# A depthwise convolution stage: Silu in one activation, taps over padded rows, another split between two engines

## The reference

```
xz = x @ in_proj_w.T
xh, z = jnp.split(xz, 2, axis=-1)
xc = jax.lax.conv_general_dilated(transpose(xh), conv_w, (1, 1), 'SAME', feature_group_count=DI)   # 3 x 3, depthwise
xc = jax.nn.silu(xc + conv_b[None, :, None, None])
x_flat = xc.reshape(B, DI, L)                              # rows after rows: U in the kernel
x_t = jnp.transpose(xc, (0, 1, 3, 2)).reshape(B, DI, L)    # columns after columns: UT
...                                                        # projections, a scan in four directions, a layer norm
y = y * jax.nn.silu(z)
return y @ out_proj_w.T
```

## Time and profile before

| | us |
|---|---|
| median of 3 runs | 4313.52 |
| lowest and highest run | 4308.7, 4328.05 |
| span of the profiled execution | 4322.2 |

### The profile page before, as it was taken

The page is one execution under the profiler, slowest core; times in us unless marked ns, Lnnn a source line. Parts: engine busy times, 40 slices in busy tenths (PEclk is TensorE's granted clock), DMA queues, the critical chain, the costliest instruction groups (busy, mean ns, idle before and its releaser), DMA issues. The chain is left out here.

```text
span 4322.2 us, 110119 instructions
## 1 busy us (share of the span) xinstructions
PE 3375.4 (78%) x46784; PEld 1688.2 (39%) x46784; DVE 3524.7 (82%) x3560; ACT 2718.5 (63%) x4416; POOL 1598.8 (37%) x1151
## 2 busy tenths in 40 slices
PE   6788873157777776317777778868999999999998
PEld 4476631012222223101222222553566566666553
DVE  5555476989999967789999996759988888888882
ACT  2365628845555544865555543534899999999995
POOL 0122220079999961009999995000000000000000
PEclk9799986568888887657888877977999999999999
DMA  5334203433232210353223321451221212222211
GB/s 130 83 67 75 54 18 91 145 79 79 71 76 71 66 49 10 112 146 74 72 65 77 76 61 39 126 153 41 56 56 56 64 56 56 64 56 56 56 41 49
DMA packets 160560, 309.95 MB, mean 72 GB/s; under 512 B 69592, under 2 KB 105752, under 8 KB 156101
## 3 DMA queue, kind: packets, MB, share of 16 engines
q1 hardware_dynamic: 159124, 301.24, 27.0%
q10 hardware_dynamic: 944, 1.67, 0.2%
HBM read 194.44 MB, written 107.83 MB: 70 GB/s over the span
## 5 line engine op out<-in xcount | busy, mean ns | idle before, releaser
L2323 DVE TENSOR_REDUCE l3a_mx<-l3a_mx 128x2 f32<-128x768 f32 x1296 | 1165.1, 952 | 160.2 <-PE l3a_mx L2222 156.1
L2289 ACT ACTIVATE l3a_p<-l3a_s 128x384 f32<-128x384 f32 x2592 | 1181.5, 492 | 113.2 <-PE l3a_s L2236 105.7
L1545 POOL TENSOR_TENSOR l_scan_sc<-l_scan_s,l_scan_repc 128x768 f32<-128x768 f32 x576 | 1032.3, 1837 | 5.9 <-DVE l_scan_s L1523 5.7
L1487 ACT ACTIVATE l_scan_da<-l_scan_da,l_k_a 128x768 f32<-128x768 f32 x576 | 503.9, 875 | 627.7 <-PE l_scan_da L1407 627.6
L2236 PE MATMUL l3a_s<-l3a_q,l3a_k 125*32 125x384 f16 x10368 | 802.1, 327 | 5.8 <-DMA l3a_q<-l3a_m 3.9
L2222 PE MATMUL l3a_mx<-l3a_k,l3a_q 124*32 124x384 f16 x10368 | 672.0, 334 | 57.4 <-DMA l3a_q<-l_qx 30.4
L1407 PE MATMUL l_scan_dup<-l_scan_du,l_k_pick 96*128 96x512 bf16 (+1 forms) x1152 | 347.2, 390 | 317.6 <-DMA l_scan_dt<-l_dtp 159.1
L2248 PE MATMUL l3a_o<-l3a_p,l3a_vh 128*32 128x288 f32 x6912 | 568.7, 405 | 0.8 <-issue 0.5
L1536 POOL TENSOR_TENSOR l_scan_bup<-l_scan_dus,l_scan_repb 128x768 f32<-128x768 f32 x192 | 352.6, 1837 | 484.6 <-DMA l_scan_repc<-l_bcp 484.6
L2190 POOL TENSOR_TENSOR l3a_norm<-l3a_out,l3a_spread 128x576 f32<-128x576 f32 x24 | 34.5, 1437 | 1342.1 <-DMA l3a_spread<-l_inverses 1342.1
L1407 PE MATMUL l_scan_da<-l_scan_dt,l_k_pick 96*128 96x512 bf16 (+1 forms) x1152 | 340.6, 384 | 156.1 <-DVE l_scan_s L1523 152.6
(11 more groups left out here) (215 smaller groups left out, 4295.3 us busy)
## 6 DMA issues: line engine op xcount, KB each, us to landing
l3a_q<-l_qx SPq DMA_DIRECT2D x96, 486.0 KB
l_scan_du<-l_dup SPq DMA_DIRECT2D x144, 144.0 KB
l_scan_dt<-l_dtp SPq DMA_DIRECT2D x138, 144.0 KB
l_scan_repb<-l_bcp SPq DMA_DIRECT2D x48, 384.0 KB
l_scan_repc<-l_bcp SPq DMA_DIRECT2D x46, 384.0 KB
l_dtp<-l_prep_high_t SPq DMA_DIRECT2D x16, 432.0 KB, 3.1
l_dup<-l_prep_high_u SPq DMA_DIRECT2D x16, 432.0 KB, 3.1
l_dtp<-l_prep_middle_t SPq DMA_DIRECT2D x16, 432.0 KB, 3.1
```

What stands on the lines that cost most here:

```text
L1487: act.activation(da_ps[st % 2][:, 0:TC], da_ps[st % 2][:, 0:TC], ACT.Exp, scale=A[:, column:column + 1]).then_inc(exped, 1)
L1545: pool.tensor_tensor(SC[:, st % NSC, :], S[:, n, :], REPC[k % 2][:], ALU.mult).then_inc(weighted, 1)
L2289: act.activation(P[:, k % NP, third * SW:(third + 1) * SW], s_ps[u % NS_PS][:, 0:SW], ACT.Exp)\
L2323: dve.tensor_reduce(MX[:, qt % (NB * KT), 2 * pair:2 * pair + 2], mx_ps[n % NR][:, :, 0:RG], AX_X, ALU.max)\
```

## The change

The stage is rewritten in four respects.

1. **Silu.** ACT's own Silu function replaces the chain of Exp, Ln and Exp. For z it reads the projected strip in PSUM and writes the gated strip. For u it reads the taps' sums and writes U, and a second Silu reads the same sums in exchanged order and writes UT, so the final copy is gone. The work is done by strip (PE's) and by unit (DVE's), not by image.
2. **Taps.** `conv` now has rows of 50 positions like `pad`, so that a DVE tap is one contiguous run of 16 x 50 - 2 = 798 positions in place of 16 rows of 48. The two positions at each row's end are computed and not used.
3. **Split.** DVE has five units (ten strips), PE two strips. POOL makes the nine diagonal matrices, and clears only the border of `pad` by four small memsets; ACT doesn't wait for them any more, DVE and PE do.
4. **Weights and stores.** The three loads move into `LateConstants.load`, ahead of its seven others, in the stage before. The stage no longer waits for the stores of U (`ssm_prepare` does, at its end), and U of the first image is stored earlier.

The core of the diff:

```diff
-            e = s.sb("e", [DI, B, L])
+        flat = s.sb("pad", [DI, B * (H + 2) * PADW])
+        pad = flat[:, :].rearrange("p (b h w) -> p b h w", b=B, w=PADW)
-        PE_STRIPS = [(1, r) for r in range(2 * PH, H, PH)]
-        DVE_UNITS = [(0, 0), (0, 2 * PH), (0, 4 * PH), (1, 0)]
+        DVE_UNITS = [(0, 0), (0, UNIT), (0, 2 * UNIT), (1, 0), (1, UNIT)]
+        PE_STRIPS = [(1, 2 * UNIT), (1, 2 * UNIT + PH)]
...
             @block.gpsimd
             def _(pool):
-                pool.memset(pad[:], 0.0).then_inc(padded, 1)
+                pool.memset(pad[:, :, 0, :], 0.0).then_inc(padded, 1)
+                pool.memset(pad[:, :, H + 1, :], 0.0).then_inc(padded, 1)
+                pool.memset(pad[:, :, 1:H + 1, 0:1], 0.0).then_inc(padded, 1)
+                pool.memset(pad[:, :, 1:H + 1, PADW - 1:PADW], 0.0).then_inc(padded, 1)
+                pool.wait_ge(loaded, 48)
+                for k in range(9):
+                    pool.tensor_scalar(diag[:, k, :], eye[0:DI, 0:DI], cw[:, k:k + 1], None, ALU.mult)\
+                        .then_inc(diag_made, 1)
...
+                def gate_z(n):
+                    b, r = strips[n]
                     act.wait_ge(z_ready, n + 1)
+                    act.activation(z[:, b, r * W:r * W + STRIP], z_ps[n % 3][:, 0:STRIP], ACT.Silu).then_inc(z_gated, 1)
+                def gate_unit(j):
+                    b, r = DVE_UNITS[j]
+                    act.wait_ge(tapped, j + 1)
+                    c = tapped_rows(b, r)
+                    act.activation(image_of(U[:, b, :])[:, r:r + UNIT, :], c, ACT.Silu).then_inc(gated, 1)
+                    act.activation(turned_home(b, r, UNIT), c.rearrange("p h w -> p w h"), ACT.Silu).then_inc(turned, 1)
+                def gate_strip(j):
+                    b, r = PE_STRIPS[j]
+                    act.wait_ge(taps_summed, j + 1)
+                    c = c_ps[j % 2][:, 0:STRIP]
+                    act.activation(U[:, b, r * W:(r + PH) * W], c, ACT.Silu, bias=cb[:, 0:1]).then_inc(strip_gated, 1)
+                    act.activation(turned_home(b, r, PH), c.rearrange("p (h w) -> p w h", w=W), ACT.Silu,
+                                   bias=cb[:, 0:1]).then_inc(strip_turned, 1)
+                unit_after = {10: 0}
+                unit_after_z = {4: 1, 10: 2}
...
                 for b, r in DVE_UNITS:
                     dve.wait_ge(placed, placed_for(b, r + UNIT))
-                    c = image_of(conv[:, b, :])[:, r:r + UNIT, :]
+                    c = conv[:, b, r * PADW:(r + UNIT) * PADW - 2]
                     for k in range(9):
-                        src = pad[:, b, r + k // 3:r + k // 3 + UNIT, k % 3:k % 3 + W]
+                        at = (b * (H + 2) + r + k // 3) * PADW + k % 3
+                        src = flat[:, at:at + UNIT * PADW - 2]
...
     def load(self, sp):
         t, pre = self.t, self.pre
+        sp.dma_start(self.cw_in[:], t[pre + "in_wT"].rearrange("(k p) n -> p k n", p=CP)).then_inc(self.conv_loaded, 16)
+        sp.dma_start(self.cw[:], t[pre + "conv_w"]).then_inc(self.conv_loaded, 16)
+        sp.dma_start(self.cb[:], t[pre + "conv_b"]).then_inc(self.conv_loaded, 16)
```

More of the change, by code:

```diff
@@ L912, in _, with place @@
             def _(pool):
-                pool.memset(pad[:], 0.0).then_inc(padded, 1)
-                for b in range(B):
-                    pool.wait_ge(z_exped, b + 1)
-                    pool.tensor_scalar(ez[:, b, :], ez[:, b, :], 1.0, E_MOST, ALU.add, ALU.min).then_inc(z_raised, 1)
+                pool.memset(pad[:, :, 0, :], 0.0).then_inc(padded, 1)
[6 more added lines that the diff above has]
+                        .then_inc(diag_made, 1)
             @block.scalar
             def _(act):
[L920 to L928, removed]
+                def place(n):
+                    b, r = strips[n]
                     act.wait_ge(x_ready, n + 1)
@@ L932, in _ @@
                        .then_inc(placed, 1)
-                act.wait_ge(loaded, 48)
-                for n, (b, r) in enumerate(strips):
+                def gate_z(n):
+                    b, r = strips[n]
                     act.wait_ge(z_ready, n + 1)
[L936 to L950, removed]
@@ L961, in _ @@
-                for b in range(B):
-                    act.wait_ge(gated, b + 1)
-                    act.activation(image_of(UT[:, b, :]), U[:, b, :].rearrange("p (h w) -> p w h", w=W), ACT.Copy)\
-                       .then_inc(turned, 1)
-                act.wait_ge(turned, B)
+                    act.activation(z[:, b, r * W:r * W + STRIP], z_ps[n % 3][:, 0:STRIP], ACT.Silu).then_inc(z_gated, 1)
[5 more added lines that the diff above has]
+                    act.activation(turned_home(b, r, UNIT), c.rearrange("p h w -> p w h"), ACT.Silu).then_inc(turned, 1)
@@ new lines, in _ @@
+                unit_after_z = {4: 1, 10: 2}
+                for n in range(n_s):
+                    if n in unit_after:
+                        gate_unit(unit_after[n])
+                    place(n)
+                for n in range(n_s):
+                    if n in unit_after_z:
+                        gate_unit(unit_after_z[n])
+                    gate_z(n)
+                gate_strip(0)
+                gate_unit(3)
+                gate_strip(1)
+                gate_unit(4)
+                act.wait_ge(turned, len(DVE_UNITS))
@@ L1074, in _ @@
                 sp.wait_ge(low_stored, 32 * UNITS)
+                sp.wait_ge(late.u_stored, 16 * B)
             @block.tensor
@@ L2429, in build @@
                         group_norm(nc, f"gn{layer}", X, XN, group_mean, preload=late.load, stats=stats)
[L2430 removed]
+                        ssm_conv(nc, pre + "conv", XN, late, U, UT, z_dram, u_dram, eye)
                     ssm_prepare(nc, pre + "prep", t, pre, U, UT, dt_dram, du_dram, bc_dram, late)
```

79 lines of the change are left out of this document (28 added, 51 removed).

## The result

| | before | after |
|---|---|---|
| median, us | 4317.34 (4 runs) | 4253.7 (4 runs) |
| lowest and highest run | 4308.7, 4328.05 | 4251.46, 4258.35 |
| span of the profiled execution | 4322.2 | 4249.7 |

The changed kernel is faster, by about 1.5 per cent: the ratio of its runs to those of before is 0.9854, with a 95% interval from 0.9833 to 0.9876. That is 63.6 us by the medians and, by the interval, between 54 and 72 us.

The account below looks back on a forecast made before the run. It took each convolution stage as a chain ending at a barrier, filled by no engine. Savings of 37.3 and 35.9 us, less 1 given back, made 72 us off 4313.5: 4241.5 us, range 4230 to 4260.

Parts of the forecast that it names:

- the forecast's own spread: Whole kernel: 4230 to 4252 us, from the units' bounds and the 10 us between timed runs of before.
- POOL in DVE's way: Rival, chance 0.14: POOL's diagonals at 1.2 us each, four falling into DVE's first unit, some 6 us a layer; 4254 us.
- no better taps: Rival, chance 0.10: tap 1.055 us, exchanged Silu 2.8 ns an element, weights 3 us late; about 7.5 us a layer, 4257.
- What bounds the stage: Convolution stage: a chain ending at a barrier, no engine filling it; 54.9 us in place of 92.26 and 90.79.
- DVE's five units set the end: End of the taps: DVE's last sums at 640.5, PE's strips at about 629.5 and 635.5, 5 us to spare.
- PE's own sum: PE in layer 1: projections through at about 623.5, under 2 us lost waiting for ACT, strips 5.85 us each.
- The size of a unit: DVE's unit of contiguous taps: 0.97 us a tap, 8.85 us a unit, 44.3 us for five.
- The upper bound: DVE's unit at most 9.5 us, from the old tap scaled by its elements, 1.055 us.
- The first tap: DVE's first tap: 7.29 us after the stage's start, at 596.24 in place of 600.62 in layer 1.
- Silu: ACT's gating: 0.82 ns an element and 0.17 us fixed; a unit's U 0.80 us, UT 1.48, together 2.3.
- Given back in the next stage: ssm_prepare: weights queue behind U's last store, 0.5 us a layer (0 to 3); Exp's table load covered by waiting.
- The total: Whole kernel: 72 us less than the 4313.5 us median, giving 4241.5 us.

Follow-up runs that it names:

- e_split: The changed kernel with the old split, four units on DVE and four strips on PE; stages 64.3 and 63.2 us against 58.56 and 57.60.
- e_imm: The changed kernel with the taps' weights and bias as numbers in the instruction, not SBUF columns (sums wrong); stages 55.26 and 55.52 us against 58.56 and 57.60.
- e_rows: The changed kernel with DVE's taps again over 16 rows of 48 in the padded layout; stages 57.22 and 56.46 us against 58.56 and 57.60.
- e_loads: The changed kernel with the three loads issued again at the convolution stage's start; stages 61.9 and 60.8 us against 58.56 and 57.60.
- e_zsilu: The kernel before with only z gated by one Silu out of PSUM; stages 87.9 and 87.4 us against 92.26 and 90.79.
- e_usilu: The kernel before with only u gated by one Silu per whole image, exchanged copy kept; stages 83.4 and 81.6 us against 92.26 and 90.79.
- e_warm: The changed kernel with unread PE products ending group_norm (four) and starting ssm_prepare (two); stages 55.6 and 57.3 us against 58.56 and 57.60.
- e_best: The changed kernel with row taps, three 24-row DVE units, three PE strips and unread PE products; stages 54.4 and 53.0 us, median 4243.9 us.

## Why the prediction was right, and where it was off

The direction and the mechanism were right, and the gain was 63.6 us in place of 72. The 4253.7 us lie above the forecast's own spread (4230 to 4252) and inside the range because this had been widened for two rivals. One of them, POOL in DVE's way, named 4254 and didn't happen; that the numbers meet is chance. The other, no better taps, had 1.055 us for a tap, and 1.046 was measured where the forecast had 0.97.

- **What bounds the stage**: right. The stage is a chain behind a barrier, and what came off it came off the whole: the stages lost 66.9 us and the rest of the program kept its length within the spread.
- **DVE's five units set the end, PE is ahead**: right, by 5.6 us (638.4 against 644.0). e_split shows the other side. PE's own sum was too short: its projections were through at 626.65 and not at 623.5, since it waited 1.78 us for ACT and the 20 products behind the wait took 8.38 us, part of them at the clock's lower level. DVE hid that.
- **The size of a unit**: the term that was off. The sum took 0.97 us for a tap, from the idea that the 75 ns between the old tap and a plain operation were its 16 rows. The trace had them in the column of weights (e_imm) and no cost of rows (e_rows). A unit takes 9.50 us in place of 8.85, five of them 3.25 us more, which is nearly all of the 3.7 us by which layer 1's stage is longer than forecast (58.6 against 54.9). The upper bound, 9.5, was just reached. In layer 2 the stage was 2.7 us longer, since the clock rose earlier there (0.77 already in the window from 2.7 to 5.7 us after the start) and the first tap with it.
- **The first tap**: 7.76 us into the stage in layer 1 and 6.80 in layer 2, against 7.29. The preload is worth 3.2 us a layer (e_loads), less than the 4.4 and 2.9 taken together.
- **Silu**: right in ACT's cost an element. The exchanged one took 1.63 in place of 1.48 us, the pair 2.38 in place of 2.3. PSUM's exchanged reads were cheaper than taken.
- **POOL in DVE's way**: didn't happen. A diagonal took 0.52 us against the 0.5 taken; the last ended at 594.1, before the first tap at 596.68. So what a diagonal costs beside the taps was not measured. The rival's own sum is not borne out by its terms either: four diagonals of 1.2 us are 4.8 us and not 6. That POOL's additions held DVE up is shown by e_zsilu, where the fourth unit is free.
- **Given back in the next stage**: PE's restart came 3.14 us after the stage's start in place of 2.93. Over all traces whose next stage has no work added it came after 3.1 to 4.3 us with the new stage and after 2.8 to 3.0 with the old, so 0.1 to 1.5 us are given back there; that it is the store ahead of the weights is likely, but not shown. DVE's first addition there came 1.5 and 0.9 us later after the start (18.4 and 17.9 against 16.9 and 17.0), but the other traces spread from 17.0 to 18.8 with the new stage and from 17.3 to 17.8 with the old, so most of that is spread. It didn't reach the next marks, where the difference is 0.1 us.
- **The total**: 4241.5 against 4253.7. Of the 12 us, 6 are the stages (73 forecast, 67 measured), 4 are the median of before, which was 4313.5 with three runs and 4317.3 with four, and the last 2 are within the runs' spread: the timed runs of before differ by 19 us, not by the 10 that the prediction says.

What each part brought, in one layer: z's Silu 4, u's 9, the split 5.7, the preload 3.3, contiguous taps -1.2, diagonals 0. That is 21 of 33.5 us, but the parts depend on each other and don't simply add up. With both Silus, u's would start behind PE's fourth strip, which ACT had copied 61.8 us after the start in e_zsilu; the two Silus and the exchanged copies took 12.1 us in e_usilu, and 1.05 to 2.4 us follow. That makes 74.9 to 76.2 us, so the two Silus together should be worth some 16 to 17 us and not 13 (an estimate; not run). The rest should be the work by strips and units in place of whole images, above all that the exchanged copy of 8.1 us no longer stands behind everything, and that the stage doesn't wait for U's last store, which SP issued only at 645.05. Neither was tried alone: both are argued, not shown. The split could bring its 5.7 only with z's chain gone, since in the kernel before ACT's queue was later than PE.

## What to carry to other kernels

Before you credit a saving to the shape of an operand, compare rows that differ in nothing else; a column of weights in SBUF cost DVE here what looked like the price of broken rows. Where a stage ends at a barrier, write down for each engine when it would be through, and price a removed wait by the second latest of them, an engine's own queue included: the largest stall in the old trace, 13.9 us, was worth 4 at most. When a program's runs differ by 10 us from layers that a change doesn't touch, measure the stage by its own marks.

## What the runs showed of the hardware

- DVE reads no faster from one run of elements than from 16 rows of 48: 1046 ns for 798 and 1015 for 768, one slope of 1.04 ns an element, up to 1415 ns for 1152.
- In the two DVE operations of a tap, each per-partition column in place of a number costs 60 ns (1046 to 986 with one, 692 to 573 with two).
- ACT pays for a wide step in SBUF on either side, 1630 ns reading and 1531 writing against 844 for 768 elements, and nothing for one in PSUM, 566 against 577 for 384 read exchanged.
- The Trainium skill, "SBUF — State Buffer" (Who interferes with whom), says that a DVE instruction with two SBUF inputs waits for the whole of a POOL instruction that reads SBUF. The two traces agree: 8002 ns for a tap beside POOL's addition, 8.37 us for all eight taps without it.
- Products that nobody needs, some 5 us of them ahead of a stage, brought PE's granted clock to 1.00 for the projections in one stage (e_warm, layer 1); in two, layer 2 of e_warm and of e_best, it was at 1.00 when the stage started, fell to 0.50 some 1 us later and was up again 3 us after that; in one it stayed at 0.50 (e_best, layer 1).
- The clock can fall behind a short wait: after 1.6 to 1.8 us in which PE waited for ACT amid z's projections, the next 20 products of 384 columns took 6.69 us in six stages, 8.38 in three and about 10 in three. After waits of 0.6 to 1.2 us (e_rows, e_imm) they took 6.69 in all four. In the changed kernel's layer 1 the granted clock was 1.00 from 616.0 to 618.4, the wait included, and 0.57 from 618.4 to 622.4.
